# A two-layer graph transformer on one core: the order of all engine lists and of the PSUM banks

## The reference

```python
q = (src @ Wq + bq).reshape(Bb, Nn, h, dh).transpose(0, 2, 1, 3)
k = (src @ Wk + bk).reshape(Bb, Nn, h, dh).transpose(0, 2, 1, 3)
scores = jnp.einsum('bhid,bhjd->bhij', q, k) / np.sqrt(dh)
attn = jax.nn.softmax(scores, axis=-1)
for r in range(Wv.shape[0]):
    v_r = (src @ Wv[r] + bv[r]).reshape(Bb, Nn, h, dh).transpose(0, 2, 1, 3)
    mask = (adj_matrix == r)[:, None]
    out = out + jnp.einsum('bhij,bhjd->bhid', attn * mask, v_r)
attn_out = out.transpose(0, 2, 1, 3).reshape(Bb, Nn, Dm) @ Wo + bo
x = _ln(src + attn_out, g1, beta1)
ff = jax.nn.gelu(x @ W1 + b1, approximate=False) @ W2 + b2
return _ln(x + ff, g2, beta2)
```

```python
e = jnp.einsum('whqd,whkd->whqk', q, k)
e = jnp.where(e >= 0, e, ALPHA * e)
attn = jax.nn.softmax(jnp.where(adj[:, None] > 0, e, NEG), axis=-1)
h = jnp.einsum('whqk,whkd->whqd', attn, v)
out = _layernorm(h, g1, b1)
out = jnp.concatenate([out, features], axis=-1) @ Wffn.T
out = _layernorm(out, g2, b2)
return out + features
```

## Time and profile before

| | us |
|---|---|
| median of three executions | 3207.07 |
| all | 3203.78 to 3213.83 |
| profiled execution, its time | 3206.77 |
| profiled execution, its span | 3204.5 |
| TensorE busy | 3100.9 (97%) |
| VectorE busy | 2602.0 (81%) |
| ScalarE busy | 2057.2 (64%) |
| GpSimd busy | 1433.0 (45%) |

### The profile page before, as it was taken

The page is one execution under the profiler, slowest core; times in us unless marked ns, Lnnn a source line. Parts: engine busy times, 40 slices in busy tenths (PEclk is TensorE's granted clock), DMA queues, the critical chain, the costliest instruction groups (busy, mean ns, idle before and its releaser), DMA issues.

```text
span 3204.5 us, 76322 instructions
## 1 busy us (share of the span) xinstructions
PE 3100.9 (97%) x28139; PEld 2711.9 (85%) x28328; DVE 2602.0 (81%) x4896; ACT 2057.2 (64%) x4303; POOL 1433.0 (45%) x1549
## 2 busy tenths in 40 slices
PE   4899999999999999999999999999999999999996
PEld 3788888888888888888888888888888888888885
DVE  3687888888888888888888888888888888888884
ACT  2566666666666666666666666666666666666664
POOL 1344454454454454454454454454454454454441
PEclk7999999999999999999999999999999999999998
DMA  4333433433433433433433433433433433433431
GB/s 110 83 80 90 105 85 89 105 86 89 104 86 89 105 86 89 105 86 89 105 86 89 104 86 89 105 86 89 103 87 89 103 87 89 104 87 89 103 84 31
DMA packets 218074, 292.76 MB, mean 91 GB/s; under 512 B 31796, under 2 KB 119479, under 8 KB 218039
## 3 DMA queue, kind: packets, MB, share of 16 engines
q1 hardware_dynamic: 218038, 292.30, 39.0%
HBM read 73.02 MB, written 16.78 MB: 28 GB/s over the span
## 4 chain that ended last, share of the span: by engine, by line
PE 88%; issue 4%; ACT 3%; DVE 2%; SPq 1%; DMA 1%; POOL 1%; POOLq 0%; DVEq 0%; ACTq 0%
PE pair L982 49%; PE pair L1012 15%; PE pair L1036 7%; PE pair L1026 6%; PE pair L1091 4%; PE pair L1100 2%; PE pair L1028 2%; ACT probs L560 2%; PE pair L1000 2%; SPq L298 1%; PE pair L987 1%; PE pair L1107 0%; POOL act_r_lo L417 0%; ACT leaky_s L539 0%; DMA stack_a<-qk 0%
## 5 line engine op out<-in xcount | busy, mean ns | idle before, releaser
L417 POOL TENSOR_TENSOR act_r_lo<-act,act_r_hi 128x512 fp32r<-128x512 f32 x256 | 335.8, 1321 | 741.1 <-DVE act_r_hi L946 538.7
L539 ACT ACTIVATE leaky_s<-leaky_s,low_r 128x256 f32<-128x256 f32 x1024 | 506.2, 499 | 2.8 <-DVE low_r L788 2.0
L423 POOL TENSOR_TENSOR probs<-probs,rel 128x512 f32<-128x512 f32 x256 | 293.7, 1170 | 211.4 <-ACT probs L560 123.4
L560 ACT ACTIVATE probs<-pair 128x1024 f32<-128x1024 f32 x256 | 256.9, 1030 | 199.0 <-PE pair L1100 199.0
L792 DVE TENSOR_REDUCE mx_a<-pair 128x4 f32<-128x1024 f32 x256 | 307.7, 1223 | 78.3 <-PE pair L1091 78.1
L533 ACT ACTIVATE leaky_s<-pair 128x1024 f32<-128x1024 f32 x256 | 262.7, 1026 | 159.5 <-PE pair L1028 159.5
L784 DVE TENSOR_TENSOR leaky_s<-pair,leaky_s 128x1024 f32<-128x1024 f32 x256 | 312.3, 1220 | 38.6 <-ACT leaky_s L533 38.4
L788 DVE TENSOR_REDUCE low_r<-leaky_s 128x4 f32<-128x1024 f32 x256 | 310.8, 1214 | 2.2
L529 ACT ACTIVATE probs<-pair 128x1024 f32<-128x1024 f32 x256 | 262.1, 1024 | 65.7 <-PE pair L1036 61.5
L423 POOL TENSOR_TENSOR leaky_s<-probs,rel 128x512 f32<-128x512 f32 x256 | 291.1, 1171 | 0.3 <-ACT probs L560 0.3
L1036 PE MATMUL pair<-ident,leaky_s 128*128 128x128 f32 x2048 | 269.3, 275 | 7.5 <-ACT leaky_s L539 6.6
(11 more groups left out here) (193 smaller groups left out, 8830.1 us busy)
## 6 DMA issues: line engine op xcount, KB each, us to landing
stack_a<-qk SPq DMA_DIRECT2D x768, 128.0 KB, 2.4
stack_r<-qk SPq DMA_DIRECT2D x768, 128.0 KB, 2.4
xt<-in_xT SPq DMA_DIRECT2D x64, 256.0 KB, 3.5
adj_a<-in_adjT SPq DMA_DIRECT2D x64, 256.0 KB, 3.0
xn<-in_x SPq DMA_DIRECT2D x64, 256.0 KB, 3.4
adj_q<-in_adj SPq DMA_DIRECT2D x64, 256.0 KB, 2.9
out<-n SPq DMA_DIRECT2D x64, 256.0 KB, 2.8
probs<-in_w SPq DMA_DIRECT2D x4, 512.0 KB, 4.6
```

Of the source, the lines that this page charges most:

```text
L417: return nc.gpsimd.tensor_tensor(dst, src, hi, ALU.subtract)
L423: last = nc.gpsimd.tensor_tensor(masked_p[g][:, h], probs[:, g, h], rel1[:], ALU.mult)
L539: last = nc.scalar.activation(leaky_s[:, p % SLOTS, k, t], leaky_s[:, p % SLOTS, k, t], ACT.Exp, bias=low_r[:, p, k, t:t + 1], accum_out=d ...
L560: return nc.scalar.activation(probs[:, g, 2 * q:2 * q + 2], pair[b][:], ACT.Exp, scale=SCALE)
```

## The change

No operation is added or removed, and no instruction has another size. The order of the calls in every `body` is another, and so are the banks and the waits that guard their reuse. The core of it on TensorE (minus is before, plus after, some waits left out):

```diff
-        B_AO, B_ADEN, B_Q, B_K, B_WO, B_X1T, B_RV, B_HN = 2, 6, 7, 6, 1, 4, 4, 2
+        B_AO, B_ADEN, B_Q, B_K, B_WO, B_X1T, B_RV, B_HN = 4, 5, 0, 2, 6, 3, 3, 3
...
                 if g1 is not None:
+                    pe.wait_ge(stacked_r[0].sem, stacked_r[0].at(g1))
+                    masked_rows(0, B_RR[0]).then_inc(sr_mm.sem, 1)
...
                     pe.wait_ge(stacked_r[3].sem, stacked_r[3].at(g1))
                     masked_rows(3, B_RR[3]).then_inc(sr_mm.sem, 1)
-                    pe.wait_ge(leaky_done.sem, leaky_done.at(g1, 3))
-                    turn(1, B_TN[1]).then_inc(turned_mm.sem, 1)
...
                 if g3 is not None:
                     pe.wait_ge(stacked_a[0].sem, stacked_a[0].at(g3))
-                    pe.wait_ge(v_done.sem, v_done.at(g3))
...
                     score_cols(2, B_AC[2]).then_inc(sta_mm.sem, 1)
-                    pe.wait_ge(probs_a.sem, probs_a.at(g3, 2))
                     if ran(g3, 2):
                         pe.wait_ge(heads_r.sem, heads_r.at(g3 - 2))
+                    score_cols(3, B_AC[3]).then_inc(sta_mm.sem, 1)
+                    pe.wait_ge(probs_a.sem, probs_a.at(g3, 2))
                     both(0).then_inc(pva_mm.sem, 1)
-                    if ran(g3, 1):
-                        pe.wait_ge(x2t_split.sem, x2t_split.at(g3 - 1))
-                    score_cols(3, B_AC[3]).then_inc(sta_mm.sem, 1)
...
+                if g2 is not None:
+                    row_products(B_LV, (x2t_hi, x2t_lo), "lv").then_inc(rv_mm.sem, 1)
                 if g3 is not None:
                     pe.wait_ge(probs_a.sem, probs_a.at(g3))
                     both(1).then_inc(pva_mm.sem, 1)
-                if g1 is not None:
-                    pe.wait_ge(n1t_split.sem, n1t_split.at(g1))
-                    half_ffn((n1t_hi, n1t_lo), 0, False).then_inc(ffn_mm.sem, 1)
-                if g2 is not None:
-                    pe.wait_ge(rqk_split.sem, rqk_split.at(g2))
-                    row_products(B_LV, (x2t_hi, x2t_lo), "lv").then_inc(rv_mm.sem, 1)
-                    pe.wait_ge(stacked_r[0].sem, stacked_r[0].at(g2))
-                    masked_rows(0, B_RR[0]).then_inc(sr_mm.sem, 1)
-                if g3 is not None:
                     pe.wait_ge(probs1_done.sem, probs1_done.at(g3, 2))
                     one(0).then_inc(pv1_mm.sem, 1)
                     pe.wait_ge(probs1_done.sem, probs1_done.at(g3))
                     one(1).then_inc(pv1_mm.sem, 1)
...
+                if g1 is not None:
+                    pe.wait_ge(n1t_split.sem, n1t_split.at(g1))
+                    half_ffn((n1t_hi, n1t_lo), 0, False).then_inc(ffn_mm.sem, 1)
```

On VectorE the count of known relations goes from between centre and rescale of LN_H to before centre of LN_M; `lowest_row(1)` from behind `leaky(1)` to behind `leaky(3)`; the maxima of a graph come in the turn of its projections. On ScalarE `exp_rows(1)` goes behind the last gelu. On GpSimd the residual, the root of LN_O and the low parts of the first two activations go to the end of the turn:

```diff
-                if g0 is not None:
-                    pool.wait_ge(ln_done[LN_M].sem, ln_done[LN_M].at(g0))
-                    if ran(g0, 1):
-                        pool.wait_ge(ln_done[LN_O].sem, ln_done[LN_O].at(g0 - 1))
-                    residual().then_inc(x2k_done.sem, 1)
                 if g1 is not None:
                     pool.wait_ge(ln_mv[LN_M].sem, ln_mv[LN_M].at(g1))
                     make_rstd(LN_M, g1)
                 if g2 is not None:
                     pool.wait_ge(probs_a.sem, probs_a.at(g2, 1))
-                    pool.wait_ge(rel1_done.sem, rel1_done.at(g2))
                     masked(0).then_inc(probs1_done.sem, 1)
```

SyncE now loads adj_a in turn -3 before the stack copies; in a turn its order is xt, shift copy, adj_q, stack_r 0 and 1, xn, stack_r 3, adj_a, stack_r 2, stack_a 0 and 1, the store, stack_a 2 and 3. In the opening VectorE's weight pieces lie between the maxima of graph 0:

```diff
+                if g3 is not None:
+                    if path.opening:
+                        other_weights()
+                    dve.wait_ge(sa_mm.sem, sa_mm.at(g3, 1))
+                    maximum(0, B_AR[0]).then_inc(mx_a_done.sem, 1)
...
+                if g3 is not None:
+                    if path.opening:
+                        weights(STAGES + FIRST_W, n_pieces - 4)
+                    dve.wait_ge(sa_mm.sem, sa_mm.at(g3, 3))
+                    maximum(2, B_AR[2]).then_inc(mx_a_done.sem, 1)
+                    dve.wait_ge(sa_mm.sem, sa_mm.at(g3))
+                    maximum(3, B_AR[3]).then_inc(mx_a_done.sem, 1)
+                    if path.opening:
+                        weights(n_pieces - 4, n_pieces - 1)
+                    dve.wait_ge(amt_mm.sem, amt_mm.at(g3))
+                    shift(bank(B_AMT)[0:H, 0, :], shift_a, g3, ashift_hi, ashift)
```

More of the change, by code:

```diff
@@ L78 @@
     general = False
+    opening = False
 def ran(graph, back):
@@ L331, in body @@
                 if g1 is not None:
+                    load(adj_q, adj, g1, "(t p) n -> p t n", ld_adj_r)
                     sp.wait_ge(rqk_split.sem, rqk_split.at(g1))
@@ L334, in body @@
                     stack(1, stack_r, stacked_r)
+                if g2 is not None:
+                    load(xn, x, g2, "(t p) c -> p t c", ld_xn)
+                if g1 is not None:
+                    stack(3, stack_r, stacked_r)
+                if g3 is not None:
+                    if ran(g3, 1):
+                        sp.wait_ge(known_done.sem, known_done.at(g3 - 1))
+                    load(adj_a, adjT, g3, "(t p) n -> p t n", ld_adj_a)
+                if g1 is not None:
                     stack(2, stack_r, stacked_r)
-                    stack(3, stack_r, stacked_r)
-                if g2 is not None:
-                    load(adj_q, adj, g2, "(t p) n -> p t n", ld_adj_r)
                 if g3 is not None:
@@ L705, in _, with last_weights @@
                                         W["wv"][0][:, :, r * D:(r + 1) * D], ALU.subtract).then_inc(ready, 1)
+            def last_weights():
+                path.opening = False
+                weights(n_pieces - 1, n_pieces)
             weights(0, FIRST_W)
@@ L841, in body @@
                     statistics(LN_M, res, g1)
-                if g2 is not None:
-                    dve.wait_ge(ld_adj_a.sem, ld_adj_a.at(g2))
-                    nc.vector.tensor_scalar(rel1[:], adj_a[:], 1, None, ALU.is_equal).then_inc(rel1_done.sem, 1)
+                if g2 is not None and not path.general:
+                    nc.vector.scalar_tensor_tensor(adj_a[:], adj_a[:], 0, rel1[:], ALU.is_equal, ALU.add,
+                                                   accum_out=known[:]).then_inc(known_done.sem, 1)
                 if g1 is not None:
                     dve.wait_ge(ln_mv[LN_M].sem, ln_mv[LN_M].at(g1))
-                    if ran(g1, 1):
-                        dve.wait_ge(x2k_done.sem, x2k_done.at(g1 - 1))
                     centre(LN_M, res, G2, x2)
@@ L868, in body @@
                     centre(LN_H, n1, LG1, n1)
-                if g2 is not None and not path.general:
-                    dve.wait_ge(rel1_done.sem, rel1_done.at(g2))
-                    nc.vector.scalar_tensor_tensor(adj_a[:], adj_a[:], 0, rel1[:], ALU.is_equal, ALU.add,
-                                                   accum_out=known[:]).then_inc(known_done.sem, 1)
-                if g0 is not None:
                     dve.wait_ge(ln_mid[LN_H].sem, ln_mid[LN_H].at(g0))
```

242 lines of the change are left out of this document (123 added, 119 removed).

## The result

The changed kernel takes 3218.87 us (median of 9 runs, 3216.44 to 3221.70) against 3207.27 of the kernel before beside it (9 runs): a ratio of 1.0034, 95% interval 1.0025 to 1.0044. It is 11.6 us slower. 3212 was predicted, with 3184 to 3245 as the range and slower as the likeliest sign. The profiled execution has a span of 3219.0 us, 14.5 more than before.

The account below looks back on a forecast made before the run. TensorE, busy 97% of the span, was taken to bound the kernel. Opening, first partial turn, entry, end and settled turns: 3206.8-9-2-2+2+16=3211.8, given as 3212 us, range 3184 to 3245.

Parts of the forecast that it names:

- TensorE at one(1): Settled turn: TensorE reaches the last masked product 12.6 us after the column scores start (S), instead of 15.36.
- Masks to end at S+13.40: Settled turn: GpSimd's four masks end 13.40 us after the column scores start, instead of 13.59.
- one(1) at S+13.48: Settled turn: the last masked product starts 0.08 after the masks end, so TensorE waits some 0.9 us every turn.
- the hold: GpSimd's second mask waits for layer 2's first norm; claimed to bind in 62 turns, +0.26 each, +16 us.
- From one(1) to the next S: Settled turn, last masked product to the next column scores: 34.86 us instead of 32.72; turn 48.34 against 48.08.
- The entry: Loop's entry turn, where x2's transpose waits 3.08 us: more to spare on that path, -2 us, from -5 to +2.
- The end: Last graph's rows: exps 1 to 3 one behind another after leaky 3, +2 us, from -1 to +4.
- Opening and first partial turn: Graph 1 starts near 70.5 instead of 79.75, -9 us; the partial turn from 79.75, -2, from -4 to +1.
- rival 2: Settled turn: masks and TensorE meet, turn falls towards 47.5; 3184 with half of it, 3157 with all; chance 0.13.
- 3 out: Rival on the opening: weights, not the order, end it, so -9 becomes near 0; 3221 us, chance 0.10.
- 4 out: Rival on TensorE's clock: it alternates with the new wait, 62 x 1.8 = 112 us; 3324, chance 0.05.
- Rival 1: A second wait, at TensorE's x1 transpose with zero spare: 0.3 a turn more, +20 us, 3232; chance 0.25.

Follow-up runs that it names:

- a_rel: The changed kernel with only VectorE's comparison of adj_a moved behind x1's rescale: 3210.80 us, ratio 1.0014.
- a_nohold_rel: The changed kernel without GpSimd's wait for layer 2's first norm and with VectorE's comparison of adj_a behind x1's rescale: 3178.67 us, ratio 0.9922.
- a_ffb: The changed kernel with the second half of the feed-forward moved back ahead of one(0): 3196.12 us, ratio 0.9967.

## Why the prediction was right, and where it was not

- **TensorE at one(1)**, S+12.6: it would have been there at S+12.63. Masks to end at S+13.40: 13.40. one(1) at S+13.48: 13.45. A wait of 0.9: 0.82. These steps stand. The added product, the removed hold and the block moved back show that the masks, late by the hold, are what makes the settled turn longer. The new banks and the place of masked_rows(0) were not tried alone.
- **From one(1) to the next S**, 34.86: 34.94. The turn is 48.39 against 48.08, +0.31 for +0.26. The 57 settled turns give 18.1 us, where the sum had 16 for 62: a term slightly too small.
- **The entry**, -2: this term failed. The entry turn did get 3.5 us shorter (52.71 to 49.20), without the wait of 3.08 for x2, as I said. But the turn from 117 got 3.9 us longer than before (51.94). Of these 3.9, 2.3 go when the comparison moves out of the way of exp 0 (a_rel has 49.69 there), so they come from the load of adj_a; the rest is not taken apart. The first four turns together give +0.4. I had read the moved load only for the stack copies behind it on SP's queue, not for the comparison that VectorE now meets earlier.
- **The end**, +2, was mis-sized: +8.7. Half of it, 4.5, lies in the last graph's way from masked_rows(0) to row_values. The step counted the exps behind leaky(3), and they cost 2.2. It left out that turn(1) now stands behind them too (2.0 at the low clock), and the half feed-forward (0.4). The other 4.5 lie ahead of that, from the last wq to the last graph's masked_rows(0): 94.4 us instead of 89.9. There turn(0) of the last graph but one waits 3.56 us where it waited 0.85, since masked_rows(0), moved behind one(1), has no work of a next graph behind it. TensorE's x1 transpose then waits 1.06 instead of 2.12; the rest of this half I did not take apart. Behind row_values the end is 0.3 shorter. More of the end runs at 1.2 GHz: the granted clock of the last 43.5 us is 0.58 where the earlier trace rows have 0.69. What that costs by itself no run shows.
- **Opening and first partial turn**, -9 and -2: -8.9 and -3.8, the second at the better end of its bounds.
- **Sum**: the terms came to +5 and are +14.5; seven tenths of the miss are the end. The range held it and the sign was the one with the most weight. In the ledger the sum misses by 9.5 us: 6.7 at the end, 2.4 at the entry, 2.1 in the turns, less 1.8 in the first partial turn. That the median came within 7 us of 3212 is in part luck, since the first partial turn took some of the miss back and the medians lie closer together than the two profiled executions.
- **Rivals.** The hold binds (rival 2 out), the opening does what it says (3 out), the clock stays (4 out). Rival 1, a second wait in every turn, did not come; VectorE takes 8.02 us from leaky(0) to the rescale, as computed, with no wait at x1's transpose. Its thought was right for the kernel without the first wait, at another place. The time of rival 2 at its far end was too low, though: I had 47.46 for the turn without the hold, and a_nohold_rel, with no flagged wait left, has 47.81. Most of that difference is the 0.26 by which TensorE comes later to one(1) beside the slow rescales.

## What to carry to other kernels

When a block is moved from ahead of a consumer to behind it, work out separately when the consumer's data are ready: here 1.5 us of feed-forward had been the cover of the masks, and moving it back gave 23 us, about as much as shortening the chain (19; with the comparison moved as well, both end at 3179). A wait that looks like a mere brake (a hold on one engine until another has written) is tried in the kernel in which it was put: the same line cost 19 us in one order and saved 25 in the other. And for each moved load or split, read the in-order queue between the two engines, not only their lists; the start and the end of the pipeline need their own sum, since what covers a step in the loop is not there.

## What the runs showed that I had not expected

- VectorE's two-input rescale beside a GpSimd product: 1.35 to 1.39 us instead of 0.48 (128x256), while the GpSimd product of 128x512 goes from 1.17 to between 1.20 and 1.30. VectorE loses 1.7 to 1.8 us a turn over two instructions, GpSimd 0.3 to 0.65 over eight.
- An idle time of 1.8 us of TensorE in every turn of 49.5 left its clock at 1.00 over 2600 us; the last 49 us of the program, with 22.9 of work, had 0.59.
- In a_ffb, VectorE waits for the load of adj_a in some settled turns, up to 1.3 us, and in most not at all, though queue and order are the same in each. Why it is late in those turns is not shown.
